# Expert rows scattered by token instead of gathered by token, in a graph, attention and expert layer stack

## What is computed

```python
xs = x.reshape(-1, m)
probs = jax.nn.softmax(xs @ Wg, axis=-1)
topv, topi = jax.lax.top_k(probs, K)                 # 8 experts, K = 2
cw = topv / jnp.sum(topv, axis=-1, keepdims=True)
...
    h = jax.nn.relu(dispatched @ W1[e] + b1[e])
    expert_outputs = expert_outputs + sel * (h @ W2[e] + b2[e])
...
combined = jnp.einsum('ks,ksm->sm', combine_weights, rerouted)
...
x = x + _L0_ffn_ref(_layernorm(x, axis=-1)[None], ...)[0]
xn = _layernorm(x, axis=-1)
```

## Time and profile before

| | us |
|---|---|
| median of 3 runs | 2831.78 (2825.46 to 2832.0) |
| the profiled execution | 2834.7 |
| its span, first to last instruction | 2832.9 |
| expert loop, from the first L1201 to the end of the last L1212 | 1206.1 to 1443.9 |
| combining loop, to the start of `down(1)` | 1443.9 to 1505.4 |

### The profile page before, as it was taken

The page is one execution under the profiler, slowest core; times in us unless marked ns, Lnnn a source line. Parts: engine busy times, 40 slices in busy tenths (PEclk is TensorE's granted clock), DMA queues, the critical chain, the costliest instruction groups (busy, mean ns, idle before and its releaser), DMA issues.

```text
span 2832.9 us, 31076 instructions
## 1 busy us (share of the span) xinstructions
PE 2698.0 (95%) x11845; PEld 1875.9 (66%) x11845; DVE 1489.6 (53%) x2309; ACT 980.1 (35%) x1596; POOL 100.8 (4%) x144
## 2 busy tenths in 40 slices
PE   6999999999989999899959999999999999999999
PEld 5786656798876556577745755566677776555555
DVE  7997889699973455511142210243876774431230
ACT  8894101478741232222221201032644442312210
POOL 1000000000000101100040000000000000000000
PEclk9999999999999999899979999999999999999999
DMA  9904221211030301399956110000200103000000
GB/s 238 332 3 92 102 68 60 71 55 54 19 72 6 94 5 51 105 383 357 359 175 138 40 34 34 1 15 1 89 30 30 30 30 124 15 11 6 11 11 11
DMA packets 131740, 238.12 MB, mean 84 GB/s; under 512 B 18639, under 2 KB 99572, under 8 KB 131118
## 3 DMA queue, kind: packets, MB, share of 16 engines
q1 hardware_dynamic: 116418, 192.97, 22.2%
q0 software_dynamic: 15200, 43.44, 4.6%
HBM read 173.10 MB, written 63.25 MB: 83 GB/s over the span
## 4 chain that ended last, share of the span: by engine, by line
PE 82%; DVE 11%; DMA 3%; issue 2%; ACT 2%; DVEq 1%; POOL 0%; SPq 0%; ACTq 0%; POOLq 0%
PE ps L939 22%; PE ps L1364 15%; PE ps L1321 14%; PE ps L1153 5%; PE ps L893 4%; PE ps L1212 4%; PE ps L1201 4%; PE ps L956 3%; DVE arena L1984 3%; DVE arena L1985 2%; PE ps L1265 2%; PE ps L1063 1%; DVE arena L1808 1%; PE ps L1254 1%; DMA arena<-in_x_dram 1%
## 5 line engine op out<-in xcount | busy, mean ns | idle before, releaser
L939 PE MATMUL ps<-arena 128*125 128x384 f32 x2112 | 697.0, 490 | 5.4 <-DVE arena L1919 3.2
L939 PEld LDWEIGHTS ps<-arena 128*125 128x125 f32 x2112 | 396.4, 189 | 282.7 <-issue 12.4
L1364 PE MATMUL ps<-arena 128*125 128x384 f32 x1280 | 414.8, 488 | 5.8 <-DVE arena L2381 5.8
L1321 PE MATMUL ps<-arena 128*128 128x312 f32 (+1 forms) x1536 | 408.2, 428 | 5.1 <-DVE arena L2381 5.1
L1321 PEld LDWEIGHTS ps<-arena 128*128 128x128 f32 x1536 | 292.4, 191 | 119.7 <-issue 7.6
L1364 PEld LDWEIGHTS ps<-arena 128*125 128x125 f32 x1280 | 241.1, 188 | 179.4 <-issue 7.8
L2381 DVE SCALAR_TENSOR_TENSOR arena<-arena 128x1250 f32<-128x1250 f32 (+3 forms) x175 | 232.0, 1347 | 94.2 <-PE ps L1321 91.8
L1376 ACT ACTIVATE arena<-ps 128x750 f32<-128x750 f32 (+6 forms) x140 | 108.2, 777 | 485.2 <-PE ps L939 199.2
L893 PE MATMUL ps<-arena 128*125 128x380 bf16 x1280 | 213.3, 328 | 10.6 <-DVE arena L1808 10.6
L1919 DVE SCALAR_TENSOR_TENSOR arena<-ps,arena 125x768 f32<-125x768 f32 x30 | 28.7, 955 | 346.5 <-PE ps L1364 292.0
L893 PEld LDWEIGHTS ps<-arena 128*125 128x125 bf16 x1280 | 173.1, 137 | 50.6 <-DVE arena L1808 13.5
(11 more groups left out here) (320 smaller groups left out, 2649.3 us busy)
## 6 DMA issues: line engine op xcount, KB each, us to landing
arena<-in_L_ffn_W_dram SPq DMA_DIRECT2D x54, 1152.0 KB, 8.6
xs_rows<-arena SPq DMA_DIRECT2D x1, 30720.0 KB, 99.5
arena<-in_kw_dram SPq DMA_DIRECT2D x24, 512.0 KB, 4.6
arena<-al_dst POOLq DMA_DIRECT2D x18, 625.0 KB, 5.0
arena<-xs_rows SPq DMA_DIRECT2D x27, 384.0 KB, 8.3
y_rows<-arena POOLq DMA_DIRECT2D x27, 384.0 KB, 6.7
arena<-in_kw_dram SPq DMA_DIRECT2D x6, 1536.0 KB, 10.0
arena<-in_x_dram SPq DMA_DIRECT2D x2, 3600.0 KB
```

The lines of the kernel that those rows point to most:

```text
L939: mm = pe.matmul(slot(g)[0:TILE, 512 * half:512 * half + HALF], xt[:, k, i * TILE:i * TILE + TILE], w[:, k, :], start=(k == 0), stop=(k == ...
L1321: mm = pe.matmul(slot(g)[:, 512 * b:512 * b + wd_], w[:, r % 2, ORDER[p], o * P:o * P + P], feat[place(f)][:, lo + b * wd_:lo + b * wd_ + ...
L1364: mm = pe.matmul(slot(g)[0:TILE, 512 * b:512 * b + HALF], fv[:, q, :], w2c[m][q][:, b * HALF:b * HALF + HALF], start=(p == 0 and q == 0), ...
```

## The change

- Each row in `xs_rows` is two words longer (ROW = 770): behind the 768 values stand the token's number plus one, and the row of its first choice. POOL writes the token numbers once (three more `iota`); DVE copies the first row number in `slots`. The buffer of the zero fill is longer too, and the fill is issued in pieces of 385 words instead of 256. Expert tiles past the last used one now read a spare block of 128 zero rows.
- `destination(n)`, new on DVE ahead of each copy out of PSUM: four small operations that make from the two words of the loaded rows the place of each result row: the token's row in one of two blocks of 1250 rows, or a spare row. SP loads tile t only when `destination(t - 3)` is done.
- POOL stores the result by an indirect DMA into the DRAM tensor `z_rows` instead of a plain one into `y_rows`. The six operations that made `ysloti` are gone.
- The 20 indirect gathers on POOL are gone. SP issues 20 plain loads of 125 consecutive rows each, in two blocks, after all stores have landed.
- The sum of the tile comes with the second addition (`accum_out`). The sum of squares comes from ACT (`squares`), in place of `bn_stats` and `bn_aggr` on DVE. ACT's order is squares, root, copy of the tile before, normalised tile; `low_rank(0)` now follows the last tile.

Left out below are the buffers' sizes, the reads of `xf` under its new layout, and two calls that now name their target tile.

```diff
@@ -56,6 +56,7 @@
+ROW = 768 + 2
@@ -394,8 +395,12 @@
-yslotf = rcut(2 * NT)[0:TILE].rearrange("p (k t) -> p k t", k=2)
-ysloti = rcut(2 * NT)[0:TILE].bitcast(I32).rearrange("p (k t) -> p k t", k=2)
+total = rcut(NT)[0:TILE]
+ssq = rcut(NT)[0:TILE]
+nmu = rcut(NT)[0:TILE]
+ptab = rcut(1)
+spare = rcut(NTAU)
+home = rcut(2)
@@ -416,21 +421,25 @@
+rowp = rcut(NTAU)
+desti = rcut(NTAU).bitcast(I32)
...
-xf = ct_r[0:TILE, 0:NT * D].rearrange("p (t d) -> p t d", t=NT)
+X0 = R_ACC + R_XT + R_CT - NT * ROW
+xf_all = arena[0:TILE, X0:X0 + NT * ROW].rearrange("p (t d) -> p t d", t=NT)
+xf = [xf_all[:, NT - 1 - t, :] for t in range(NT)]
...
-xs2 = [aa_r[:, 9216 + D * n:9984 + D * n] for n in range(ERING)]
+xs2 = [aa_r[:, 9216 + ROW * n:9216 + ROW * n + ROW] for n in range(ERING)]
...
-xs_d = nc.dram_tensor("xs_rows", (EXP * ROOM, D), F32).ap()
-y_d = nc.dram_tensor("y_rows", (NTAU * TAU, D), F32).ap()
+xs_d = nc.dram_tensor("xs_rows", (EXP * ROOM + TAU, ROW), F32).ap()
+z_d = nc.dram_tensor("z_rows", (1 + 2 * NODES + NTAU * TAU, D), F32).ap()
@@ -598,8 +607,8 @@
-    load(xs_d.rearrange("(p q) (c n) -> p (q c) n", p=P, c=3),
-         zero16.bitcast(F32).unsqueeze(1).broadcast_to([P, 3 * EXP * ROOM // P, 256]), "xs_zero")
+    load(xs_d.rearrange("(p q) (c n) -> p (q c) n", p=P, c=2),
+         zero16.bitcast(F32).unsqueeze(1).broadcast_to([P, 2 * (EXP * ROOM + TAU) // P, ROW // 2]), "xs_zero")
@@ -651,7 +660,8 @@
-        r = sp.value_load(rowi[0:1, t:t + 1], min_val=0, max_val=EXP * ROOM - TAU)
+            sp.wait_ge(ev("dest"), t - ERING + 1)
+        r = sp.value_load(rowi[0:1, t:t + 1], min_val=0, max_val=EXP * ROOM)
@@ -669,6 +679,12 @@
+    for q in range(3):
+        sp.wait_ge(ev(f"y_out{q}"), 16 * len(range(q, NTAU, 3)))
+    for t in range(NT):
+        for k in range(2):
+            lo = 1 + k * NODES + t * TILE
+            sp.dma_start(back[k][t], z_d[lo:lo + TILE]).then_inc(ev(f"back{t}"), 16)
@@ -823,6 +839,13 @@
+    pool.wait_ge(ev("A_in"), (HEADS + 1) * NT)
+    own.step(pool.iota(ptab, [[0, 1]], base=0, channel_multiplier=1,
+                       allow_small_or_imprecise_dtypes=True))
+    own.step(pool.iota(spare, [[TAU, NTAU]], base=1 + NODES, channel_multiplier=1,
+                       allow_small_or_imprecise_dtypes=True))
+    own.step(pool.iota(xf_all[:, :, D], [[-TILE, NT]], base=1 + (NT - 1) * TILE, channel_multiplier=1,
+                       allow_small_or_imprecise_dtypes=True))
@@ -831,18 +854,14 @@
-                                    in_=xf[:, t, :], in_offset=None).then_inc(ev("scattered"), 16)
+                                    in_=xf[t], in_offset=None).then_inc(ev("scattered"), 16)
...
-        pool.dma_start(y_d[n * P:n * P + P], yb[n % 3]).then_inc(ev(f"y_out{n % 3}"), 16)
+        pool.wait_ge(ev("dest"), n + 1)
+        pool.indirect_dma_start(out=z_d, out_offset=bass.IndirectOffsetOnAxis(ap=desti[:, n:n + 1], axis=0),
+                                in_=yb[n % 3], in_offset=None).then_inc(ev(f"y_out{n % 3}"), 16)
...
-    pool.wait_ge(ev("b1t"), 1)
-    for t in range(NT):
-        for k in range(2):
-            pool.indirect_dma_start(out=back[k][t], out_offset=None, in_=y_d,
-                                    in_offset=bass.IndirectOffsetOnAxis(ap=ysloti[:, k, t:t + 1], axis=0))\
-                .then_inc(ev(f"back{t}"), 16)
@@ -1587,20 +1606,25 @@
+    def squares(i):
+        act.wait_ge(ev("centred"), i + 1)
+        act.activation(H[:, i, :], acc[:, i, :], ACT.Square, bias=nmu[:, i:i + 1], accum_out=ssq[:, i:i + 1])\
+           .then_inc(ev("squared"), 1)
...
-        root_of(i)
...
-    normalised(0)
-    for i in range(NT):
-        if i + 1 < NT:
-            normalised(i + 1)
-        turned_tile("x3", i, xT)
-        if i == 6:
-            act.wait_ge(ev("u_ones"), 1)
-            low_rank(0)
+    for i in range(NT):
+        squares(i)
+        root_of(i)
+        if i >= 1:
+            turned_tile("x3", i - 1, xT)
+        normalised(i)
+    turned_tile("x3", NT - 1, xT)
+    act.wait_ge(ev("u_ones"), 1)
+    low_rank(0)
@@ -2219,6 +2243,7 @@
+        chain(dve.tensor_copy(xf[i][:, D + 1:D + 2], slotf[:, 0, i:i + 1]))
@@ -2264,9 +2289,11 @@
-    chain(dve.tensor_scalar(rowf, rowf, FULL - 1.0, float(TAU), ALU.min, ALU.mult))
+    chain(dve.tensor_scalar(rowf, rowf, float(FULL), float(TAU), ALU.min, ALU.mult))
...
+    dve.wait_ge(ev("choice_zero"), 1)
+    chain(dve.tensor_scalar(rowp, rowf, ptab[:, 0:1], None, ALU.add))
@@ -2275,29 +2302,40 @@
-    chain(dve.scalar_tensor_tensor(out=posf, in0=begin[0:TILE].unsqueeze(1).broadcast_to([TILE, NT, EXP]),
-                                   scalar=float(TAU), in1=pref, op0=ALU.mult, op1=ALU.add))
-    for k in range(2):
-        chain(dve.scalar_tensor_tensor(out=ptmp, in0=rank, scalar=float(k), in1=posf, op0=ALU.is_equal,
-                                       op1=ALU.mult))
-        chain(dve.tensor_reduce(yslotf[:, k, :], ptmp, AXX, ALU.add))
-    chain(dve.tensor_copy(ysloti, yslotf))
...
+    def destination(n):
+        dve.wait_ge(ev(f"xs_{n % ERING}"), 16 * (n // ERING + 1))
+        token, first = xs2[n % ERING][:, D:D + 1], xs2[n % ERING][:, D + 1:D + 2]
+        own.step(dve.tensor_scalar(home[:, 0:1], first, rowp[:, n:n + 1], float(NODES), ALU.not_equal, ALU.mult))
+        chain(dve.tensor_scalar(home[:, 1:2], token, 0.0, spare[:, n:n + 1], ALU.is_equal, ALU.mult))
+        chain(dve.scalar_tensor_tensor(out=home[:, 0:1], in0=home[:, 0:1], scalar=home[:, 1:2], in1=token,
+                                       op0=ALU.add, op1=ALU.add))
+        dve.tensor_copy(desti[:, n:n + 1], home[:, 0:1]).then_inc(ev("dest"), 1)
+        dve.wait_ge(ev("dest"), n + 1)
...
+        destination(n)
...
-    def lowered(i, n):
-        dve.wait_ge(ev("std"), n)
+    def varied(i):
+        dve.wait_ge(ev("squared"), i + 1)
+        dve.tensor_scalar(stdv[:, i:i + 1], ssq[:, i:i + 1], 1.0 / D, LN_EPS, ALU.mult, ALU.add)\
+           .then_inc(ev("var"), 1)
+        norms[0] += 1
+    def lowered(i):
+        dve.wait_ge(ev("std"), norms[0])
...
-        dve.scalar_tensor_tensor(out=nmean[:, i:i + 1], in0=mv[:, i, 0:1], scalar=-1.0, in1=rstd[:, i:i + 1],
-                                 op0=ALU.mult, op1=ALU.mult).then_inc(ev("shifted"), 1)
+        dve.tensor_tensor(nmean[:, i:i + 1], nmu[:, i:i + 1], rstd[:, i:i + 1], ALU.mult)\
+           .then_inc(ev("shifted"), 1)
@@ -2307,18 +2345,22 @@
-    counted = []
...
-        for k in range(2):
-            chain(dve.scalar_tensor_tensor(out=acc[:, t, :], in0=back[k][t], scalar=share[:, k, t:t + 1],
-                                           in1=acc[:, t, :], op0=ALU.mult, op1=ALU.add))
-        counted.append(statistics(t, acc))
+        own.step(dve.scalar_tensor_tensor(out=acc[:, t, :], in0=back[0][t], scalar=share[:, 0, t:t + 1],
+                                          in1=acc[:, t, :], op0=ALU.mult, op1=ALU.add))
...
-            lowered(t - 1, counted[t - 1])
-    lowered(NT - 1, counted[NT - 1])
+            varied(t - 1)
+        own.settle()
+        chain(dve.scalar_tensor_tensor(out=acc[:, t, :], in0=back[1][t], scalar=share[:, 1, t:t + 1],
+                                       in1=acc[:, t, :], op0=ALU.mult, op1=ALU.add, accum_out=total[:, t:t + 1]))
+        if t >= 1:
+            lowered(t - 1)
+        dve.tensor_scalar(nmu[:, t:t + 1], total[:, t:t + 1], -1.0 / D, None, ALU.mult).then_inc(ev("centred"), 1)
+        dve.wait_ge(ev("centred"), t + 1)
+    varied(NT - 1)
+    chain(dve.tensor_scalar(mv[:, :, 1], ssq, 1.0 / D, None, ALU.mult))
+    lowered(NT - 1)
```

More of the change, by code:

```diff
@@ L322, in build @@
         off8 = ecut(SPREAD)
-        zero16 = ecut(256).bitcast(BF16)
+        zero16 = ecut(ROW // 2).bitcast(BF16)
         base = ecut(NB + 1)
@@ L1124, in turn_input @@
                     o = slot(g)[:, 512 * (k // 3) + TILE * (k % 3):512 * (k // 3) + TILE * (k % 3) + TILE]
-                    mm = pe.transpose(o, xf[:, i, k * P:k * P + P], ident[0:TILE, 0:TILE])
+                    mm = pe.transpose(o, xf[i][:, k * P:k * P + P], ident[0:TILE, 0:TILE])
                 ready(mm)
@@ L1909, in normal @@
                 chain(dve.reciprocal(rstd[:, i:i + 1], stdv[:, i:i + 1]))
-                dve.tensor_scalar(dst[:, i, :], src[:, i, :], mv[:, i, 0:1], rstd[:, i:i + 1],
+                dve.tensor_scalar(dst, src[:, i, :], mv[:, i, 0:1], rstd[:, i:i + 1],
                                   ALU.subtract, ALU.mult).then_inc(ev("ln_" + s), 1)
@@ L1937, in _ @@
                     counted.append(statistics(i + 1, acc))
-                normal("xn", i, counted[i], acc, H)
+                normal("xn", i, counted[i], acc, H[:, i, :])
             exps = [0]
@@ L2243, in _ @@
                 emptied(dve, "agg2", j)
-                normal("xf", j, statistics(j, acc), acc, xf)
+                normal("xf", j, statistics(j, acc), acc, xf[j][:, 0:D])
             slots(NT - 2)
@@ L2378, in _ @@
                 norms[0] += 1
-                normal("at", i, norms[0], H, H)
```

(3 more changed lines are left out.)

## The result

| kernel | median, us | runs | ratio to the kernel before (95% interval) |
|---|---|---|---|
| before | 2829.7 (2825.46 to 2834.34) | 7 | 1 |
| changed | 2840.35 (2838.28 to 2843.06) | 7 | 1.0033 (1.0023 to 1.0044) |

The account below looks back on a forecast made before the run. PE carries 82% of the chain, DVE bounds the old combining loop, and DMA would bound the new one. Expert loop 0 plus combining loop 19.0 on 2834.7 gives 2853.7, or 2851 us against the median; range 2841 to 2873.

Parts of the forecast that it names:

- 20 loads on 5 engines, 62 us: Combining loop: each plain 125-row load runs on 5 of 16 DMA engines, 3.1 us each, 62 us for twenty.
- The rate of the three early loads: Three queued loads of the same shape at 34 to 35 us: 134 GB/s, the 2.87 us bound for a load.
- the store: The last store of 125 rows: 20 engine-us on five engines, the 4.0 us bound for a load.
- Rival A: Combining loop: plain loads spread over all 16 engines, tiles some 3.65 us apart, 2829 us, no measurable change; chance 0.12.
- The last scatter, 5.3 us: End of the expert loop: the last result's scatter lands 5.3 us after issue, between bounds of 2.60 and 9.0.
- Half of the pair: Two earlier scatters with 7.4 us of traffic; one was taken as half of that after 1.6 us.
- Behind the last rows, 10.1 us: Combining loop's end: from the last rows' landing to the start of `down(1)`, 10.1 us.
- the tail: From the last expert copy to `down(1)`: its start moves from 1505.43 to 1524.4 us, 19.0 us later.
- The expert loop at nothing: Expert loop: `destination`, later loads and scattered stores fit beside PE's work and cost 0 us.
- rival B: Expert loop: DMA engines cannot take the scattered rows, 0.38 us on each of 27 tiles, 2861 us; chance 0.06.
- The zero fill at nothing: Early stretch: zero fill, `iota` and extra copy lie beside PE's work far ahead, with no cost.

Follow-up runs that it names:

- e1: The changed kernel with each of the 20 loads of 125 rows cut into 120 and 5 rows: 2816.64 us, ratio 0.996.
- e5: The changed kernel with its 20 plain loads of 125 rows issued on POOL's queue instead of SP's: 2817.97 us, ratio 0.9958.
- e7: The changed kernel with loads of 128 rows instead of 125, only the very last cut into 120 and 5: 2815.94 us, ratio 0.9946.
- e2: The changed kernel with its zero fill in aligned pieces of 256 words, into a padded flat tensor: 2845.68 us, ratio 1.0066.
- e3: The kernel before with its zero fill in pieces of 385 words (1540 bytes), nothing else changed: 2821.79 us, ratio 0.9978.
- e12: The kernel before with zero fill pieces of 1024 bytes from 128 partitions, each beginning 4 bytes off in DRAM: 2851.56 us, ratio 1.0074.
- e8: The kernel before with its zero fill in aligned pieces of 1536 bytes instead of 1024: 2829.46 us, ratio 0.9996.
- e9: The kernel before with its zero fill in aligned pieces of 1024 bytes, but from 121 partitions: 2851.99 us, ratio 1.0071.

## Why the prediction was right in sign and wrong in size

1. **20 loads on 5 engines, 62 us: right.** Taken as 3.1 us a load; the tiles are 6.10 us apart, 3.05 a load, at 125 GB/s. The last tile's rows were there at 1501.31, 69.1 us after the last copy, where I had put 70.4. The rate of the three early loads was the right row to price it from, and the store the wrong end. Rival A's condition, 16 engines, is what e1, e5 and e7 made true; then the time is 12 us below A's 2829: A had none of the fill's 6.4 us, its tiles were 3.65 us apart and not 3.49 (copy to `down(1)` 58.5 us against 56.3 in e1), and it stood on the higher median.
2. **The last scatter, 5.3 us: mis-sized.** It landed in 3.0, near the lower bound of 2.60. Half of the pair in the earlier trace rows was no fair measure, since two scatters share the engines there. That is 2.3 us too much. The 20 loads with the start of the first took 64.5 us from there instead of 63.6, which takes one back.
3. **Behind the last rows, 10.1 us: right**, 9.74 measured. So the tail came to 17.3 instead of 19.0 us, and e2 has it as 17.5 between medians.
4. **The expert loop at nothing: right.** PE's distance between the two kernels stays within 0.2 us through all 27 tiles; rival B did not happen. DVE is busy 1.69 of 9 us and not 0.96, so `destination` costs it 0.73 us a tile, where I had 0.8.
5. **The zero fill at nothing: the step that failed.** The prediction says "Zero fill, `iota` and the extra copy in `slots` lie beside PE's work far ahead" and gives it no term in the sum. The fill does lie beside PE's work, but the work that hid it was slowed by it. With the new pieces, 8.4 us of the early stage go away, 6.4 between medians (e3). I had counted the longer rows by their bytes, a quarter of a per cent more, and not asked whom the fill's old form held up. The kernel before shows it: register loads of 1014 ns up to 115 us and of 310 ns from 143 us on, and PE busy 65.71 of 70 us.
6. The remaining 2 us, beside 1.7 of the tail and 6.4 of the fill, of the difference between 2851 and 2840.35 are the base: the kernel before had a median of 2829.7 beside the changed one, and 2831.78 in the runs shown ahead.

## What to carry to other kernels

A transfer's row count is a performance setting: on SP's queue 125 rows ran on 5 engines at 125 GB/s, and 128 rows (395 GB/s), or 120 and 5 (261), or the same 125 from POOL's queue (243), at a DMA share of 0.98 to 1.02. Why the three rates differ was not tried. When a change touches a large background transfer, compare in the trace of before the stretch beside it with the one behind it, the sequencers' register loads too, and don't stop at its bytes. And a change of which the sum is a small loss can hold a gain beside a larger loss, here 6.4 us against 17.5: with the loads alone mended (e1), +10.7 us became -11.5.

## What the hardware showed that I had not expected

- A plain store from SBUF whose pieces begin 4 bytes off is far slower than its bytes say: from 60 to 130 us pieces of 1024 bytes took 47 ns each aligned (kernel before) and 119 ns off (e12), pieces of 1540 bytes 110 ns (changed kernel) to 124 (e3), and aligned ones of 1536 bytes 67 (e8). The Trainium skill, "DMA: Bandwidth & Descriptors", section on how a descriptor splits into AXI transactions, has an unaligned descriptor pay for the bytes between the 256-byte boundary and its start, which are fetched and not used. For 1024 bytes that begin 4 bytes off, I estimate by its table 33 beats of 32 bytes in place of 32, some 3% more. Here, where the unaligned side is written, a piece took 2.5 times as long, so the measurement decides, and what the rest is stays open.
- DVE's register load from SBUF takes 0.31 us alone, 1.00 to 1.02 beside an aligned fill at 338 to 364 GB/s, 1.17 beside an aligned one at 164, and 0.32 beside unaligned ones at 154 to 241. e12 against the kernel before, with e2 for the one piece more, shows that the beginning of the pieces decides; e9 shows that the rate alone does not. By what path a store holds up a register load stays open: no run tried another source or another target of the store.
- 121 partitions did not give 11/16 of the rate, 240 GB/s, but 164 and less, at a share of 0.61. That too is open: no other run used a count of partitions other than 128 for the fill.
- The sum that `accum_out` brings costs DVE an instruction of 0.08 us, ACT one of 0.19.
